# A block of FFN, attention and FFN on one core: where the attention's first score units stand among the first FFN's work

## The reference

```
x = x + 0.5 * ffn(layernorm(x))
x = x + attention_block(layernorm(x))
x = x + 0.5 * ffn(layernorm(x))

ffn(h):    gamma = softmax(h @ w_router.T + b_router)      # 8 experts
           mask  = the 2 largest of gamma, per token        # 0 or 1
           y     = sum over experts of mask[e] * (h @ w_experts[e].T + b_experts[e])
attention_block(t):  q, k, v = split(t @ w_qkv), 16 heads of 16
           s = q @ k.T / 4, causal
           o = softmax(s) @ v
           return layernorm(o @ w_proj + b_proj + t) * ln_gamma + ln_beta
```

## Time and profile before

| | |
|---|---|
| timed runs | 1007.57, 1008.99, 1012.28 us; median 1008.99 |
| profiled execution | 1006.76 us, of which the span is 1005.0 |
| TensorE | busy 956.5 us (95%) |
| VectorE | busy 831.5 us (83%) |
| ScalarE | busy 511.8 us (51%) |
| GpSimd | busy 264.9 us (26%) |
| first FFN, slots 4 to 7 | 154.9 to 310.4 us |
| its close, up to the first exponential scores | 310.4 to 339.5 us |
| attention, one group | 28.0 us |

### The profile page before, as it was taken

How to read it: one execution, slowest core, us unless ns; L and a number is a source line. 1 busy time by engine, 2 the same in 40 slices (tenths; PEclk the granted TensorE clock), 3 DMA queues, 4 the chain that set the end, 5 groups by cost and what they waited for, 6 DMA issues and landing times.

```text
span 1005.0 us, 17657 instructions
## 1 busy us (share of the span) xinstructions
PE 956.5 (95%) x5602; PEld 569.3 (57%) x5602; DVE 831.5 (83%) x2445; ACT 511.8 (51%) x1053; POOL 264.9 (26%) x288
## 2 busy tenths in 40 slices
PE   6899998988998899999999999999998999999998
PEld 4678886766766433333333333333343777777776
DVE  6677777777677799999999999999868888888775
ACT  4235434414133577777777777777765333232310
POOL 1012204202021622121212212121443543435211
PEclk9999999999999999999999999999999999999999
DMA  6301121101032422222222223223320111110001
GB/s 214 98 1 64 57 70 64 58 6 63 1 95 65 139 77 66 67 71 68 70 67 71 77 77 77 76 76 77 69 84 12 44 64 64 63 49 16 19 22 42
DMA packets 55109, 64.32 MB, mean 64 GB/s; under 512 B 13824, under 2 KB 37360, under 8 KB 55024
## 3 DMA queue, kind: packets, MB, share of 16 engines
q1 hardware_dynamic: 54432, 62.47, 21.9%
q10 hardware_dynamic: 592, 0.80, 0.2%
HBM read 41.30 MB, written 21.23 MB: 62 GB/s over the span
## 4 chain that ended last, share of the span: by engine, by line
PE 65%; DVE 5%; ACT 2%; POOL 1%; issue 1%; DVEq 0%; ACTq 0%; POOLq 0%
PE bank L362 21%; PE bank L1581 14%; PE bank L1404 13%; PE bank L1565 13%; PE bank L836 2%; ACT b_probs L1544 1%; PE bank L354 1%; POOL b_ks L1377 1%; POOL a_part L496 1%; DVE c_acc L1049 1%; DVE c_st L317 1%; DVE bank L1431 0%; PE bank L785 0%; DVE c_eq L1010 0%; PE bank L1397 0%
## 5 line engine op out<-in xcount | busy, mean ns | idle before, releaser
L1544 ACT ACTIVATE b_probs<-bank 128x512 f32<-128x512 f32 (+1 forms) x608 | 302.4, 585 | 110.4 <-PE bank L1565 110.1
L1431 DVE CUSTOM_DVE_ANT_0 bank<-bank,b_below 128x384 f32<-128x384 f32 (+3 forms) x512 | 235.4, 516 | 11.1 <-PE bank L1404 9.7
L1404 PE MATMUL bank<-b_ks,b_qs 96*128 96x512 bf16 (+3 forms) x768 | 222.0, 330 | 16.4 <-DVE b_neg L1431 8.8
L1565 PE MATMUL bank<-b_qs,b_ks 99*128 99x512 bf16 (+3 forms) x768 | 214.5, 330 | 4.5 <-ACT b_probs L1544 4.3
L362 PE MATMUL bank<-we,a_xt 128*128 128x512 f32 x768 | 194.5, 405 | 0.9 <-DVE a_acc L1049 0.9
L362 PE MATMUL bank<-we,c_xt 128*128 128x512 f32 x768 | 186.2, 398 | 1.1 <-DVE c_acc L1049 0.9
L1515 POOL TENSOR_SCALAR_AFFINE_SELECT b_probs<-b_probs 128x512 f32<-128x512 f32 x128 | 84.3, 659 | 323.1 <-ACT b_probs L1544 320.0
L1435 DVE TENSOR_REDUCE b_neg<-bank 128x1 f32<-128x512 f32 x256 | 161.1, 680 | 2.6 <-PE bank L1404 1.2
L362 PEld LDWEIGHTS bank<-we,c_xt 128*128 128x128 f32 x768 | 142.3, 188 | 33.6 <-DVE c_acc L1049 2.0
L362 PEld LDWEIGHTS bank<-we,a_xt 128*128 128x128 f32 x768 | 142.7, 191 | 28.7 <-DVE a_acc L1049 1.4
L1581 PE MATMUL bank<-b_probs,b_vs 128*32 128x512 f32 (+3 forms) x1536 | 155.7, 500 | 1.2 <-POOL b_probs L1515 1.2
(11 more groups left out here) (136 smaller groups left out, 925.7 us busy)
## 6 DMA issues: line engine op xcount, KB each, us to landing
b_qs<-q_parts SPq DMA_DIRECT2D x96, 128.0 KB, 3.0
b_ks<-k_parts SPq DMA_DIRECT2D x96, 128.0 KB, 3.0
q_parts<-a_part SPq DMA_DIRECT2D x16, 384.0 KB, 2.6
k_parts<-a_part SPq DMA_DIRECT2D x16, 384.0 KB, 2.7
att_num<-b_oev SPq DMA_DIRECT2D x64, 64.0 KB, 2.2
c_num<-att_num SPq DMA_DIRECT2D x8, 512.0 KB
c_rec<-att_rec SPq DMA_DIRECT2D x16, 256.0 KB
out<-xs SPq DMA_DIRECT2D x7, 512.0 KB, 3.2
```

What stands on the lines that cost most here:

```text
L1404: last = nc.tensor.matmul(ms[bank][:, a * width:(a + 1) * width], qs[g.u][0:ROWS, c, i * P:(i + 1) * P], ks[g.u][0:ROWS, c, lo:lo + width] ...
L1431: last = dve.tensor_tensor_reduce(part, part, below[:, CH - width:CH], -1.0, 3.0e38, ALU.add, ALU.min, dst[:, a, :])
L1544: act.activation(probs[b % 4][:, heads[0]:heads[0] + hp, 0:width], es[exp_bank(g, unit)][:, 0:hp * width].rearrange("p (h w) -> p h w", w= ...
L1565: last = nc.tensor.matmul(es[exp_bank(g, unit)][:, a * width:(a + 1) * width], ks[g.u][:, c, j * P:(j + 1) * P], qs[g.u][:, c, first_q:fir ...
```

## The change

Units stand behind all eight banks of chunk 4's first two tiles, and behind 15 of chunk 7's banks instead of 16 (none behind bank 8). All positions below 47 go in turn to `pb` and `pr`, and each waits only for the last but one to be read. Since `pb` is used, the first unit of a slot also waits for the copy of the first bias, and the unit behind bank 9 for that of the second. In slots 4 to 7 `turn2` and the first bank of tile 2 stand ahead of the second bias, the router behind that, and both wait for the reads of the units of tiles 0 and 1. In slot 7 units 39, 40 and 41 and `turn2(7)` stand between and behind the four projections of chunk 6; units 47 to 49 move from slot 8 into group 0, whose `FIRST_MAXIMA` add up to 45 instead of 42. GpSimd fills group 1's ones between chunk 6's low parts. The last two `qk_mid` of chunk 7 move behind exponentials 1 and 3 of group 0; TensorE waits for the last rests at the first `products` and ScalarE for two stores each ahead of key blocks 2 and 3.

```diff
@@ -47,11 +47,11 @@
-EARLY = {NCH - 4: range(1, 8), NCH - 3: range(1, 8), NCH - 2: range(8), NCH - 1: range(16)}
+EARLY = {NCH - 4: range(8), NCH - 3: range(1, 8), NCH - 2: range(8), NCH - 1: (*range(8), *range(9, 16))}
 EARLY_FROM = {c: sum(len(EARLY[b]) for b in EARLY if b < c) for c in (*EARLY, NCH)}
-FIRST = (39, 42, 47, 50)
+FIRST = (38, 39, 40, 42, 47)
@@ -62,7 +62,7 @@
 MAXIMA = (3, 3, 2, 3, 5, 4, 4, 3, 4, 3, 4, 1)
-FIRST_MAXIMA = (6, 3, 2, 3, 5, 4, 4, 3, 4, 3, 4, 1)
+FIRST_MAXIMA = (6, 4, 3, 4, 6, 4, 4, 3, 4, 3, 3, 1)
 LAST_MAXIMA = (3, 3, 2, 2, 3, 3, 3, 3, 2, 1, 0, 0)
@@ -490,8 +490,8 @@
-        def low_parts(m):
-            for j in range(4):
+        def low_parts(m, which=range(4)):
+            for j in which:
                 pool.wait_ge(q.qk_mid, at(4 * m + j + 1))
@@ -526,12 +526,16 @@
                     pool.wait_ge(q.qk_lo, at(4 * (NCH - 1)))
-                    pool.wait_ge(q.ffn_bank, at(16 * NCH))
-                    a.ones_keys(pool, 1, 3)
                     pool.wait_ge(q.v_bank, at(2 * NCH))
                     a.ones_values(pool, 1, 5)
-                if exists(c - 1):
+                if isinstance(c, int) and c == NCH - 1:
+                    low_parts(c - 1, (0, 1))
+                    pool.wait_ge(q.qk_lo, at(4 * (c - 1) + 2))
+                    pool.wait_ge(q.ffn_bank, at(16 * NCH))
+                    a.ones_keys(pool, 1, 3)
+                    low_parts(c - 1, (2, 3))
+                elif exists(c - 1):
                     low_parts(c - 1)
@@ -685,18 +689,32 @@
                 v_out(c - 1)
-                closing = isinstance(c, int) and c == NCH - 1
-                if closing:
+                if isinstance(c, int) and c == NCH - 1:
                     spread2(c)
-                for j in (0, 2):
-                    if closing and j:
-                        split2(c)
-                    qk_hi(c - 1, j)
-                    if closing and not j:
-                        norm2(c)
-                    qk_hi(c - 1, j + 1)
-                    qk_mid(c - 1, j)
-                    qk_mid(c - 1, j + 1)
+                    qk_hi(c - 1, 0)
+                    norm2(c)
+                    qk_hi(c - 1, 1)
+                    qk_mid(c - 1, 0)
+                    split2(c)
+                    qk_mid(c - 1, 1)
+                    qk_hi(c - 1, 2)
+                    qk_hi(c - 1, 3)
+                    qk_mid(c - 1, 2)
+                    qk_mid(c - 1, 3)
+                elif exists(c):
+                    for j in (0, 2):
+                        qk_hi(c - 1, j)
+                        qk_hi(c - 1, j + 1)
+                        qk_mid(c - 1, j)
+                        qk_mid(c - 1, j + 1)
+                else:
+                    qk_hi(c - 1, 0)
+                    qk_hi(c - 1, 1)
+                    qk_mid(c - 1, 0)
+                    qk_mid(c - 1, 1)
+                    qk_hi(c - 1, 2)
+                    qk_hi(c - 1, 3)
+                    s.last_mid = lambda j: qk_mid(NCH - 1, j)
@@ -800,6 +818,9 @@
                         pe.wait_ge(q.maskt_ready, at(c + 1))
+                        pe.wait_ge(q.bias_ready, at(2 * c + 1))
+                    if (t, n) == (2, 1):
+                        pe.wait_ge(q.bias_ready, at(2 * c + 2))
                     a.first_scores(pe, position, position + 1)
@@ -818,9 +839,9 @@
-        def queries_keys(m, c):
+        def queries_keys(m, c, which=range(4)):
             pe.wait_ge(q.lo2_ready, at(m + 1))
-            for j in range(4):
+            for j in which:
                 ring_wait(pe, c, 16 + j)
@@ -856,26 +877,38 @@
                 experts(c, par, 1)
-            if exists(c + 1):
+            spread_units = first and isinstance(c, int) and c in EARLY
+            if exists(c + 1) and not spread_units:
                 router(c + 1, 1 - par)
-            if first and exists(c - 1):
+            if first and exists(c - 1) and exists(c):
                 turn2(c - 1)
-            if first and not exists(c):
-                pe.wait_ge(q.bias_ready, at(2 * NCH))
-                a.first_scores(pe, FIRST[0], FIRST[1])
-            if exists(c):
+            if spread_units:
+                experts(c, par, 2, (0,))
+                pe.wait_ge(a.mread, at(EARLY_FROM[c] + sum(n < 8 for n in EARLY[c])))
+                bias(c, par, 1)
+                if exists(c + 1):
+                    router(c + 1, 1 - par)
+                experts(c, par, 2, (1, 2, 3))
+            elif exists(c):
                 bias(c, par, 1)
                 experts(c, par, 3)
-            if first and exists(c - 1):
+            if first and isinstance(c, int) and c == NCH - 1:
                 values(c - 1)
-                if isinstance(c, int) and c == NCH - 1:
-                    a.first_scores(pe, FIRST[0] - 1, FIRST[0])
+                a.first_scores(pe, FIRST[0], FIRST[1])
+                queries_keys(c - 1, c, (0, 1))
+                a.first_scores(pe, FIRST[1], FIRST[2])
+                queries_keys(c - 1, c, (2,))
+                turn2(c)
+                queries_keys(c - 1, c, (3,))
+                a.first_scores(pe, FIRST[2], FIRST[3])
+            elif first and exists(c - 1):
+                values(c - 1)
                 if not exists(c):
-                    a.first_scores(pe, FIRST[1], FIRST[2])
+                    a.first_scores(pe, FIRST[3], FIRST[4])
                 queries_keys(c - 1, c)
@@ -930,10 +963,9 @@
         if first:
-            pe.wait_ge(q.qk_rest, at(4 * (NCH - 1) + 1))
-            a.first_scores(pe, FIRST[2], FIRST[3])
             pe.wait_ge(q.v_ready, at(2 * NCH))
-            pe.wait_ge(q.qk_rest, at(4 * NCH))
+            pe.wait_ge(q.qk_rest, at(4 * (NCH - 1) + 2))
+            s.qk_rest = q.qk_rest
@@ -1111,18 +1143,17 @@
                 stats2(c)
-                a.first_reads(dve, FIRST[0] - 1, FIRST[0])
+                a.first_reads(dve, FIRST[0], FIRST[1])
                 scale2(c)
-                qk_rests(c - 1, (0, 1))
-                a.first_reads(dve, FIRST[0], FIRST[1] - 1)
+                qk_rests(c - 1, (0,))
+                a.first_reads(dve, FIRST[1], FIRST[2])
+                qk_rests(c - 1, (1,))
                 split2(c)
-                a.first_reads(dve, FIRST[1] - 1, FIRST[1])
+                a.first_reads(dve, FIRST[2], FIRST[3])
                 qk_rests(c - 1, (2, 3))
-                a.first_reads(dve, FIRST[1], FIRST[2])
+                a.first_reads(dve, FIRST[3], FIRST[4])
             elif first and exists(c - 1):
                 qk_rests(c - 1)
-            if first and not exists(c):
-                a.first_reads(dve, FIRST[2], FIRST[3])
@@ -1333,7 +1364,7 @@
-        left = [(first_stream[n], n, first_bank(n)) for n in range(FIRST[3], len(first_stream))] if g.n == 0 else []
+        left = [(first_stream[n], n, first_bank(n)) for n in range(FIRST[-1], len(first_stream))] if g.n == 0 else []
         return left + [(entry, *place(g, n)) for n, entry in enumerate(stream(g))]
@@ -1441,17 +1472,12 @@
-        if position < FIRST[0]:
-            return 0
-        return (position - FIRST[0]) % 2 if position < FIRST[2] else position % 3
+        return (position + 1) % 2 if position < FIRST[-1] else position % 3
         for position in range(lo, hi):
-            if position <= FIRST[0]:
-                pe.wait_ge(mread, at(position))
-            elif position < FIRST[2]:
-                pe.wait_ge(mread, at(position - 1))
+            pe.wait_ge(mread, at(position - 1))
             max_scores(pe, first_stream[position], position, first_bank(position))
@@ -1532,8 +1558,8 @@
             for b, (j, half, start, width) in enumerate(keys):
-                if (g.n, b) == (0, 2):
-                    for one in s.qk_stored:
+                if g.n == 0 and b in (2, 3):
+                    for one in s.qk_stored[2 * b - 4:2 * b - 2]:
                         act.wait_ge(one, at(16 * NCH))
@@ -1544,6 +1570,8 @@
                                    ACT.Exp, scale=SCALE).then_inc(expd, 1)
+                    if (g.n, b) == (0, 0) and n % 2:
+                        s.last_mid(2 + n // 2)
                 if b == 1 and exists(g + (-1)):
@@ -1577,6 +1605,8 @@
                 pe.wait_ge(o_copied, at(2 * g.n - 1 + half))
+            if (g.n, b) == (0, 0):
+                pe.wait_ge(s.qk_rest, at(4 * NCH))
             for c in range(GH):
```

## The result

The changed kernel takes 996.08 us, the median of 4 executions (993.53 to 999.77), against 1009.74 for the kernel before (1007.57 to 1012.28): ratio 0.9864, 95% interval 0.9837 to 0.9891. Forecast were 996.2 us and a range of 990.5 to 1004. Timed again it took 995.86 us, ratio 0.9873 (0.9851 to 0.9895).

A forecast was written before the change was run, and what follows sets the result against it. TensorE, busy 95% of 1005.0 us, was taken as bound, with 21.2 us idle in five stretches to win. Terms 1.0 - 1.8 + 3.7 + 4.9 + 2.5 + 2.5 = 12.8 us took 1008.99 to 996.2 us, range 990.5 to 1004.

The forecast's parts named there:

- The bound: Slots 4 to 7 and the stretch behind: only their 21.2 us of TensorE idle time, plus clock loss, can be won.
- Two banks and the router, slots 5 to 7: Alternating unit banks and a later router remove TensorE's stalls: 3.7, 4.9 and 2.5 us won in slots 5, 6, 7.
- (b): Slots 4 to 6: VectorE becomes the bound and two banks only move the stall; 4.9 us won, 1004.1; chance 0.15.
- (d): Slots 5 to 7: late bias copy behind the logits' copy delays VectorE's tile 2; slower, 1009 to 1014; chance 0.05.
- Slot 4: First unit waits 3.0 us for GpSimd's mask; 1.0 us gained at full clock, 1.8 us set against it for a clock drop.
- rival (a): Slot 4: the clock holds behind the mask wait; 14.6 us won, 994.4 us; chance 0.20.
- The tail: Slot 7 behind the experts, slot 8 and group 0: earlier projections, reads and exponentials; 2.5 us won.
- 2.2 to 2.8 reach group 0's end: Tail: of TensorE's 4.7 us gain, VectorE's reads let 2.2 to 2.8 through to group 0's end; 2.5 taken.
- Rival (c): Tail gives nothing, as group 1's or group 2's loads come late; 10.3 us won, 998.7 us; chance 0.12.
- The sum: Whole kernel: 1.0 - 1.8 + 3.7 + 4.9 + 2.5 + 2.5 = 12.8 us won, 996.2 us from the median.

The follow-up runs named there:

- slots' part alone: Only the first FFN's part of the diff (slots 4 to 7) on the kernel before, closing order as before: 994.42 us, ratio 0.9857.
- after again: The changed kernel, unaltered, timed and profiled once more against the kernel before: 995.86 us, ratio 0.9873.
- one bank: Changed kernel with early units in one bank and no bias waits, router in its new place: 1008.42 us, ratio 0.999 to the kernel before.
- old router: Changed kernel with router, second transposes and second bias in old order in slots 4 to 7, units in two banks: 1003.88 us, ratio 0.9933 to before.
- even spread: Changed kernel with group 0's 45 maxima units spread evenly over its key blocks: 996.70 us, ratio 0.9861 to the kernel before.
- units back: Changed kernel with units 47 to 49 back in slot 8 and group 0's numbers as before (42 units): 998.89 us, ratio 0.9884 to before.
- middle parts in place: Changed kernel with ScalarE's last two middle parts of chunk 7 back ahead of all exponentials: 995.96 us, ratio 0.9854 to the kernel before.
- slots' part with the mask: Kernel before with only the first FFN's part of the diff, GpSimd's mask made ahead of chunk 2's low parts: 993.30 us, then 992.83.
- mask ahead: Changed kernel with GpSimd's mask made ahead of chunk 2's low parts instead of behind them: 995.70 us, ratio 0.9857 to the kernel before.
- the tail alone: Changed kernel with units, bias and router in slots 4 to 7 as before: 1008.03 against 1008.05 us for the kernel before, ratio 0.9996.

## Why the prediction was right, and where it wasn't

*The bound.* Right: what was won in slots 4 to 7 is their idle time and the clock's loss behind it, and the slots' part alone has the whole 13.6 us, of which its profile puts 11.7 into these slots.

*Two banks and the router, slots 5 to 7.* Right in mechanism, place and size (-3.7, -5.1, -3.3 for -3.7, -4.9, -2.5), and steady: slot 5 took 36.84 to 36.87 us in every profile with both parts. Slots 6 and 7 gave more. The rows show two differences from my count: in slot 6 no wait was left where I had kept 0.5 us before the second bias, and in both the bias copy delays the first unit by 1.15, not 1.4. The 0.8 us that slot 7 gave beyond its term are not explained by that alone. Rivals (b) and (d) are out. What the sum hid is that the terms depend on each other. I counted the router's wait at 1.31 us; behind two banks it is 1.8.

*Slot 4.* The wait of 3.0 us is 2.84, and the forecast that the clock falls behind it was luck in the profile of after: in eight profiles with this wait the slot's mean clock fell in four (after, slots alone, one bank, old router) and stayed at 1.00 in four (after again, the even spread, units back, middle parts in place), each with 39.48 us where 39.7 was counted. So the 0.20 that I gave rival (a), that the clock holds, was too low. In after its cost is 1.6 us (41.06 less 39.48), counted 1.8. The Trainium skill (TensorE: Matmul & The Clock Gate, Part 1) gives the clock two levels and lets it rise only by activity; the two levels are what the rows show (1.00, and 0.51 in the row of 327 to 334 us below), the cause of a rise is tested by no run here. The rule that the prediction took from that part of the page was found on waits of 3 to 5 us, longer than the 2.84 here, and should not have been carried over: half of the equal waits were followed by a drop.

*The tail.* Wrong, in three steps. The values of chunk 7 started 13.2 us behind the last unit, not 12.6 (13.1 before), as `split2` waits for the last projection wherever `turn2` stands. The read of unit 47 came 26.7 to 27.6 us behind it, where 26.0 was counted and 28.2 measured before: 0.6 to 1.5 us earlier, not 2.2. The exponentials did begin early, 17.5 and 16.8 us ahead of before in the two profiles, where 15.6 were forecast. But then "2.2 to 2.8 reach group 0's end" failed: with its 45 units packed into the first blocks group 0 takes 30.7 us instead of 29.4, by the runs with other pacing a matter of their order. That is 1.3 us; 1.8 more came in the first profile (32.48), where TensorE, after the wait of 2.17 us at the start of this part, ran at its lower level for 7 us:

```profile
327.00:334.00 7.00, 6.84 (x28) 2.43 (x28) 5.37 (x16) 3.32 (x7) 2.38 (x3) 0.51 0.25 84
```

VectorE, the bound of this stretch by my reading, is busy only 5.37 of these 7 us: at the lower clock TensorE is the bound. I had set the clock's loss there at nothing, though the row of before has 0.94 there. Rival (c) named this outcome, a tail that gives nothing, with group 2's late loads as the cause; the loads cost at most 0.25 us in after, and 3.3 us in another order.

*The sum.* 12.8 us were forecast, 13.7 and then 12.2 timed, though a term of 2.5 us was empty. The four slots gave 11.7 us in the first profile and 13.3 in the second, against 10.3 counted. That the total is so near is partly chance: the slots gave 1.4 and 3.0 us more than their terms, the tail 4.1 and 2.9 less.

*The rest.* Behind group 0 the kernels do the same work, and still the rest took 637.7 and 637.9 us in the two profiles of after, 636.3 in the slots' part with the mask and 635.4 in the slots' part alone. The granted clock of the last attention groups goes with it. From 700 to 760 us, in after, with the mask, and in the slots' part alone:

```profile
700.00:760.00 60.00, 54.77 (x357) 20.91 (x358) 42.85 (x112) 44.06 (x94) 22.41 (x22) 0.94 0.24 64
```

```profile
700.00:760.00 60.00, 53.56 (x359) 21.48 (x358) 44.63 (x110) 44.24 (x95) 24.46 (x23) 0.97 0.24 64
```

```profile
700.00:760.00 60.00, 53.41 (x377) 21.41 (x370) 45.40 (x114) 45.25 (x97) 24.93 (x24) 1.00 0.24 64
```

TensorE has the same wait for ScalarE there in after (1.81 us, until 715.43) and in the slots' part alone (1.82, until 715.32), and the lower clock follows in after only. So 2 us between two executions can come from a place that no edit touches, and 1.7 of the 12.7 us by which the profile of the slots' part is shorter than that of before are of this kind. Why equal waits end differently stays open.

## What to carry to other kernels

Where a producer waits for the reader of one small buffer, look at how late the reader starts in each stage: here VectorE began 4.3 us into every slot, and one more bank and one piece of other work behind the last unit gave 13 us together, against 6.7 and next to nothing alone. Undo parts one at a time and in pairs before giving each a price. Work that is moved to start an engine earlier pays only if what bounds the next stage moves too; and when a stage is bound by one engine, a lower clock of another can still change the bound, as from 327 to 334 us here. Before two executions are compared, compare their granted clock stretch by stretch, also where they do the same.

## What the runs showed that I had not expected

Equal waits of TensorE of 2.83 to 2.85 us went with a lower clock in four of eight executions, and in the execution of before, of a wait of 2.45 and one of 2.46 us, only the first did. The length of the wait alone doesn't decide it: at the start of group 0 a wait of 1.19 us with the mask ahead was followed by about 7 us at the lower level (326.7 to 333.5 us), and waits of 1.19 and 1.20 us in four other executions (after again, the tail alone, one bank, middle parts in place) by none. Nor is the stretch of one length: about 7 us in the first profile of after (327 to 334 us), between 3 and 4 us behind the wait of 2.45 us before (242.5 to 246 us). The same stretch of 45 reads took 30.69 us in three kernels to the last digit, so with a full clock differences of 0.1 us can be read from single profiles there, while whole executions differ by 3 us.
